# Gated cross-attention block: attention written out and prepared group by group, its values and softmax sums in 32-column tiles, the first router moved into the attention

## The reference

```
x = x + tanh(g_xattn) * attention(layernorm(x), ctx)     # 16 heads of 8 features, softmax over the 77 context tokens
x = x + tanh(g_ffn)   * moe(layernorm(x))

def moe(cur):                                            # 4 rounds, 4 experts, 2 of them weighted per token
    for r in range(4):
        logits = cur @ Wg[r] + bg[r]
        cw     = softmax over the two largest logits, 0 for the other experts
        hmid   = gelu(cur @ W1[e] + b1[e])               # 128 -> 512, for each expert e
        y      = hmid @ W2[e] + b2[e]                    # 512 -> 128
        cur    = cur + sum over e of cw[e] * y[e]
```

## Time and profile before

| | us |
|---|---|
| median of 3 runs (lowest, highest) | 546.52 (546.14, 546.67) |
| the profiled execution, its time | 545.69 |
| its span, first to last instruction | 544.0 |
| busy PE, DVE, ACT, POOL | 498.3, 408.1, 370.6, 79.0 |

### The profile page before, as it was taken

How to read it: one execution, slowest core, us unless ns; L and a number is a source line. 1 busy time by engine, 2 the same in 40 slices (tenths; PEclk the granted TensorE clock), 3 DMA queues, 4 the chain that set the end, 5 groups by cost and what they waited for, 6 DMA issues and landing times.

```text
span 544.0 us, 8396 instructions
## 1 busy us (share of the span) xinstructions
PE 498.3 (92%) x2529; PEld 401.7 (74%) x2529; DVE 408.1 (75%) x792; ACT 370.6 (68%) x717; POOL 79.0 (15%) x149
## 2 busy tenths in 40 slices
PE   0967989999679999999999999999999999999996
PEld 0845777777568788878878887887888788788884
DVE  3789888988955887786688778768877876876775
ACT  1434566556466788597778859777885977787873
POOL 3375565664400000000000000000000000000000
PEclk9985999999988999999999999999999999999999
DMA  5500000000004040021003001200400120040001
GB/s 133 162 2 0 2 0 0 0 0 0 2 0 157 0 157 1 1 77 80 2 1 155 2 0 69 89 2 0 157 1 1 74 84 0 1 175 2 19 1 39
DMA packets 13063, 22.39 MB, mean 41 GB/s; under 512 B 5200, under 2 KB 9957, under 8 KB 10981
## 3 DMA queue, kind: packets, MB, share of 16 engines
q1 hardware_dynamic: 9648, 21.42, 10.8%
q10 hardware_dynamic: 3381, 0.55, 0.6%
HBM read 20.79 MB, written 1.18 MB: 40 GB/s over the span
## 4 chain that ended last, share of the span: by engine, by line
PE 68%; DVE 13%; ACT 9%; issue 6%; DMA 2%; ACTq 1%; DVEq 0%
PE ps L1121 8%; PE ps L1123 8%; PE ps L1122 8%; PE ps L1103 8%; PE ps L1102 8%; PE ps L1101 8%; PE ps L1015 7%; ACT g_sb L590 4%; DVE h_lo L801 4%; PE ps L993 4%; PE ps L1002 3%; ACT h_hi L597 2%; ACT probT L507 2%; DMA rows_in<-in_L_xattn_bkv_dram 1%; PE ps L949 1%
## 5 line engine op out<-in xcount | busy, mean ns | idle before, releaser
L801 DVE TENSOR_TENSOR h_lo<-g_sb,h_hi 128x512 fp32r<-128x512 f32 x256 | 170.5, 688 | 88.1 <-ACT h_hi L597 88.1
L590 ACT ACTIVATE g_sb<-ps,cols 128x512 f32<-128x512 f32 x256 | 174.7, 689 | 60.4 <-PE ps L1103 60.0
L597 ACT ACTIVATE h_hi<-g_sb 128x512 fp32r<-128x512 f32 x256 | 154.8, 634 | 0.0
L1121 PE MATMUL ps<-h_hi,w_hi 128*128 128x512 f32 x256 | 103.3, 404 | 0.0
L1101 PE MATMUL ps<-x_hi,w_hi 128*128 128x512 f32 x256 | 101.9, 398 | 0.8 <-DVE x_lo L795 0.8
L1103 PE MATMUL ps<-x_hi,w_lo 128*128 128x512 f32 x256 | 102.1, 399 | 0.0
L1123 PE MATMUL ps<-h_hi,w_lo 128*128 128x512 f32 x256 | 102.0, 399 | 0.0
L1102 PE MATMUL ps<-x_lo,w_hi 128*128 128x512 f32 x256 | 101.4, 396 | 0.0
L1122 PE MATMUL ps<-h_lo,w_hi 128*128 128x512 f32 x256 | 101.3, 396 | 0.0
L811 DVE SCALAR_TENSOR_TENSOR contrib<-ps,cols,cwb 128x512 f32<-128x512 f32 x64 | 47.8, 746 | 13.6 <-PE ps L1123 8.4
L1101 PEld LDWEIGHTS ps<-x_hi,w_hi 128*128 128x128 f32 x256 | 48.5, 189 | 12.4 <-issue 1.0
(11 more groups left out here) (129 smaller groups left out, 503.3 us busy)
## 6 DMA issues: line engine op xcount, KB each, us to landing
cwb<-cw_rows SPq DMA_DIRECT2D x16, 1024.0 KB, 5.9
x_sb<-in_x_dram SPq DMA_DIRECT2D x4, 256.0 KB, 9.1
w_in<-in_L_ffn_W_dram SPq DMA_DIRECT2D x1, 1024.0 KB, 8.0
out_dram<-xn SPq DMA_DIRECT2D x4, 256.0 KB, 2.3
ctx_sb<-in_ctx_dram ACTq DMA_DIRECT2D x1, 462.0 KB
cw_rows<-cwT SPq DMA_DIRECT2D x8, 16.0 KB, 1.4
wq_in<-in_L_xattn_Wq_dram SPq DMA_DIRECT2D x1, 64.0 KB, 2.7
bv_row<-in_L_xattn_bkv_dram ACTq DMA_DIRECT2D x1, 64.0 KB, 9.7
```

The lines of the kernel that those rows point to most:

```text
L590: nc.scalar.activation(g_sb[:, k, :], ps[:, k, :], ACT.Gelu_apprx_tanh, bias=b1_c[:, e * NF + k:e * NF + k + 1]).then_inc(gelu_done, 1)
L597: nc.scalar.activation(h_hi[:, u % 2, k, :], g_sb[:, k, :], ACT.Copy).then_inc(hi_done, 1)
L801: nc.vector.tensor_tensor(h_lo[:, u % 2, k, :], g_sb[:, k, :], h_hi[:, u % 2, k, :].bitcast(F32), ALU.subtract).then_inc(lo_done, 1)
L1121: mm(yb, w2_hi[:, w], hh, start=k == 0, stop=False)
```

## The change

- Preparation goes by groups of four sequences. Only group 0 is prepared ahead; the work for group c = 1, 2, 3 is dealt out over the four iterations b of the group before (r = b % 4): r = 0 transposes of `ctx`; r = 1 K and the transposes of the normalised x; r = 2 Q and a third of V; r = 3 the other two thirds of V. Second normalisations, their transposes, `split_x` of groups 0 and 1 and the whole first router stand in iterations 5 to 15.
- V no longer goes through `pick`: PE multiplies `ctxT` (each row twice) by 16 columns of the weights per head group, four 64-column float32 matmuls for each of three row chunks (`project_v`, new L995), and DVE masks 256 columns into `v_st` (`stage_v`, new L686).
- A head group of 308 score columns has three chunks of 103, 103 and 102 rows: 12 transposes a sequence. Values and softmax sums are 24 float32 matmuls a sequence, each of 32 columns, into a column tile of its own (`weigh_values`, new L1041 and L1046; the sums use the 0/1 matrix `row_head`). The reduction, the small reciprocal, the widening, its transpose and its copy are gone; in their place is one reciprocal of 128 columns (new L710).
- The loop is written out, and the pipeline is one sequence shorter on DVE: iteration b shifts the scores of b and normalises b-1.
- SP loads the first group of x ahead of the projection matrices; ACT's queue loads `rows_in` (with one row more) ahead of `ctx`, which is in four parts. POOL adds the output bias to x sequence by sequence. The expert part is as before, but for the router of units 8 to 15, which is up to two units later, and all later copies of router weights, one unit later.

```diff
-            with pe.Fori(1, B // 2 - 1) as j:
-                attend(2 * j, 0)
-                attend(2 * j + 1, 1)
...
+            for b in range(B):
+                c, r = b // TC + 1, b % TC
+                if b + 1 < B:
+                    scores(b + 1, 0)
+                if b >= 1:
+                    weigh_values(b - 1)
+                transpose_probs(b, 0)
...
+                if c < NC:
+                    if r == 0:
+                        transpose_ctx(c)
+                    if r == 1:
+                        project_k(c)
+                    if r == 2:
+                        project_q(c)
+                    if r == 3:
+                        project_v(c, 1)
+                if b + 1 < B:
+                    scores(b + 1, 1)
+                transpose_probs(b, 1)
+                transpose_probs(b, 2)
+                if b >= 1:
+                    project_o(b - 1)
...
+                if c < NC:
+                    if r == 1:
+                        transpose_xn(c)
+                    if r == 2:
+                        project_v(c, 0)
+                    if r == 3:
+                        project_v(c, 2)
+                if r == TC - 1 and c >= 2:
+                    transpose_x(c - 2)
+                if b == B - 3:
+                    logits(0)
+                if b == B - 1:
+                    transpose_weights(0)
```

```diff
+            def weigh_values(b):
...
+                for k in range(KC):
+                    n = rows_of[k]
+                    for q in range(NQ):
+                        mm(acc(b)[32 * q:32 * q + 32, 0:L], v_st[0:n, c % 2, k, b % TC, q, :],
+                           probT[0:n, KC * q + k, :], start=k == 0, stop=k == KC - 1)
+                for k in range(KC):
+                    n = rows_of[k]
+                    for q in range(NQ):
+                        t = mm(acc(b)[32 * q:32 * q + 32, L:2 * L], row_head[0:n, k, :, :].rearrange("p h d -> p (h d)"),
+                               probT[0:n, KC * q + k, :], start=k == 0, stop=k == KC - 1)
+                t.then_inc(pv_done, 1)
```

DVE in the new iteration (its waits: `low_q` for ACT's `q_hi`, `stage_v` for PE's V, `normalise_o` for `pv_done`):

```diff
+                shift(b, 0)
+                if b >= 2:
+                    add_residual(b - 2)
...
+                if c < NC and r == 2:
+                    low_q(c)
+                if c < NC and r == 3:
+                    stage_v(c, 1)
+                shift(b, 1)
+                if b >= 1:
+                    normalise_o(b - 1)
...
+                if c < NC and r == 2:
+                    stage_v(c, 0)
+                if c < NC and r == 3:
+                    stage_v(c, 2)
+                if r == 3 and 1 <= c < NC - 1:
+                    moments(0, c + 1)
+                if r == 1 and c >= 2:
+                    moments(1, c - 2)
+                if r == 0 and c >= 3:
+                    split_x(c - 3)
...
+                if r == 0 and c < NC:
+                    normalise(0, c)
+                if r == 2 and c >= 2:
+                    normalise(1, c - 2)
+                if b == B - 3:
+                    router(0)
+                if b == B - 2:
+                    weights(0)
```

More of the change, by code:

```diff
@@ new lines, in flamingo_gated_block, with next_job, moved @@
+        turn = [0]
+        def next_job(key, reader):
+            job(key, reader, TB + turn[0] % 2)
+            turn[0] += 1
+        for b in range(B):
+            first, second = between(b)
+            next_job(("PT", b, 0), "act")
+            for key, reader in first:
+                next_job(key, reader)
+            next_job(("PT", b, 1), "act")
+            next_job(("PT", b, 2), "act")
+            for key, reader in second:
+                next_job(key, reader)
+        def moved(eng, key):
+            reader, n = jobs[key][1:3]
+            if reader == "act":
+                eng.wait_ge(job_act, n)
+            elif reader == "dve":
+                eng.wait_ge(job_dve, n)
+            elif reader == "router":
+                eng.wait_ge(gate_step, 2)
+            else:
+                eng.wait_ge(cwT_moved, 1)
@@ L708, in _, with shift @@
             mx_v = mx[:, :].rearrange("p (q h) -> p q h", q=NQ)
-            def shift(b, half, first=False):
+            def shift(b, half):
                 two = slice(2 * half, 2 * half + 2)
@@ L760, in _ @@
-            moved(dve, JOBS - 1)
-            dve.wait_ge(xres_step, 2)
-            shift(0, 0, first=True)
-            shift(0, 1, first=True)
-            attend(0, 0, values=False, residual=False)
-            attend(1, 1, residual=False)
-            with dve.Fori(1, B // 2 - 1) as j:
-                attend(2 * j, 0)
-                attend(2 * j + 1, 1)
-            attend(B - 2, 0, queries=False)
-            attend(B - 1, 1, scores=False, queries=False)
-            for c in range(NC - 1):
-                dve.wait_ge(x1_done, TC * (c + 1))
-                moments(x1_sb, 1, c)
@@ L887, in finish @@
                     op0=ALU.mult, op1=ALU.add).then_inc(fin_done, 1)
[L889 to L891 removed]
+            moments(0, 0)
+            dve.wait_ge(c_ready, 3)
+            nc.vector.tensor_reduce(head_mask[:, :], head_at[:, :, :].rearrange("p q h -> p h q"), AX.X,
+                                    ALU.add).then_inc(headmask_ready, 1)
+            normalise(0, 0)
+            moments(0, 1)
+            moved(dve, "COLS")
+            low_q(0)
@@ L982, in scores, with transpose_ctx @@
-            def scores(b, s, half, first=False):
+            tr(bank("W")[:, 0:P], wq_in[:, :], ident[:, :])
+            tr(bank("W")[0:C, P:2 * P], wk_in[:, :], ident[:, :])
+            tr(bank("W")[0:C, 2 * P:3 * P], wv_in[:, :], ident[:, :])
+            tr(bank("W")[:, 3 * P:4 * P], wo_in[:, :], ident[:, :]).then_inc(job_mm, 1)
+            pe.wait_ge(rows_ld, 16 * 5)
+            tr(bank("COLS")[:, 0:NCOL], rows_in[:, :], ident[0:NCOL, 0:NCOL]).then_inc(job_mm, 1)
+            def transpose_ctx(c):
+                key = ("CTX", c)
+                claim(key)
+                pe.wait_ge(ctx_ld[c], 16)
+                for t in range(TC):
+                    m = tr(bank(key)[0:C, t * M:(t + 1) * M], ctx_sb[:, TC * c + t, :], ident[0:M, 0:M])
+                m.then_inc(job_mm, 1)
@@ L984, in scores @@
+            passes = ((q_hi, k_hi), (q_hi, k_lo), (q_lo, k_hi))
+            def scores(b, half):
+                c, at = b // TC, slice(b % TC * L, b % TC * L + L)
                 if half == 0:
-                    pe.wait_ge(q_lo_done, b + 1)
+                    moved(pe, ("Q", c))
                     pe.wait_ge(k_stage, 3 * b + 3)
-                if not first:
+                if b >= 1:
                     pe.wait_ge(sub_done, 2 * b - 1 + half)
-                passes = ((q_hi, k_hi), (q_hi, k_lo), (q_lo, k_hi))
```

973 lines of the change are left out of this document (457 added, 516 removed).

## The result

| | us |
|---|---|
| before, median (lowest, highest), 4 runs | 546.33 (545.48, 546.67) |
| after, median (lowest, highest), 4 runs | 595.03 (592.66, 597.88) |
| ratio, 95% interval | 1.0896 (1.0846 to 1.0946) |
| profiled execution of after, its time and span | 592.66, 590.9 |
| first maximum, before and after | 41.87, 17.02 |

The change makes the kernel 9% slower. The forecast was 598. The page of the kernel after: busy times, then the rows of busy tenths and of the granted clock in 40 slices of 14.8 us.

A forecast was written before the change was run, and what follows sets the result against it. PE was busy 92%, DVE 75%, but in-order waits were taken to decide. Span 544.0, plus 37.1 for a later `up(2)` and 15 for slow clock, gave 596; with execution and median offsets, 598 us, range 560 to 645.

The forecast's parts named there:

- The mechanism: Attention loop: DVE waits for b-1's products before `shift(b + 1, 0)`, so nothing of it hides PE; 10.5 us per sequence, not 6.0.
- V = 2.8: Attention: a sequence's 24 column-tile products of values and sums take 2.8 us, overlapping only at tile borders.
- the signs named ahead: Attention trace: DVE idle before three operations, DVE and PE under 70%, iterations 7 to 9 or 12 to 14 us, `up(0)` near 192.
- The start: Before the attention: `rows_in` lands at 14.35, first maximum begins at 22.7 instead of 41.87; gain 19 us.
- The rival of tiles wholly at once: Attention values: four column tiles fully overlap, 1.4 us a sequence; time 577, or 562 without slow clock; chance 0.25.
- about 2.0: Attention values: by the skill's 2.38 gain for three column tiles, about 2.0 us a sequence, sum some 12 us lower.
- The reciprocal: Attention, DVE: the new 128-column reciprocal takes 1.0 us, from a slope giving 0.8 to 1.2.
- The clock: Attention: PE waits drop it to 1.2 GHz for a fifth of its chain, 15 us; bounds none to 74.
- the forecast's chain: Start through attention to `up(2)`: serial waits and operations at full clock put `up(2)` at 203.5, 37.1 later than before.
- The tail: Experts from `up(2)` on: both kernels do the same, 5.96 us a unit; later router weights cost nothing.
- The other side: Attention: queues do not bind, each sequence costs the fullest engine's 7.1 us; `up(2)` at 149, time 529; chance 0.10.
- the turning point: Attention: below a mean of 8.1 us an iteration, `up(2)` would come before 166.4 and the change be faster.

The follow-up runs named there:

- e7: After with preparation evictions behind `shift` halves, first router behind `shift(14, 0)`, and 57 unused PE products where PE idles ahead of scores: 530.38 us.
- e2: After with `low_q` and all `stage_v` evictions moved behind the halves of `shift` on DVE, PE's program unchanged: 548.26 us.
- e5: After with only the evictions ahead of `shift(b, 1)` (`low_q`, `stage_v(c, 1)`, `stage_v(0, 0)`) moved behind it: 573.68 us.
- e6: After with only the evictions ahead of `shift(b + 1, 0)` (`stage_v(c, 0)`, `stage_v(c, 2)`, `stage_v(0, 1)`, `stage_v(0, 2)`) moved behind it: 569.97 us.
- e1: After in its own order, with 94 extra unused float32 products on PE where it waits for DVE: 576.53 us.
- e9: e7 with `weights(0)` moved behind `shift(15, 1)` and 2 in place of 6 unused products at b = 14: 529.12 us.
- e3: After with the two loops of `weigh_values` exchanged, so one column tile's products follow each other: 601.44 us in one run.
- e10: e7 with the two loops of `weigh_values` exchanged, one column tile at a time, clock held: 545.43 us.

## Why the prediction held, step by step

The forecast of 598 lies 0.5% above 595.03, and its direction and place were right. Its sum was less good than that: errors of 28 us one way met 33 the other way.

**The mechanism: right.** The forecast said that nothing of `shift(b + 1, 0)` hides PE, since DVE cannot go past what waits for PE, and that r = 2 and 3 would be the long iterations. Predicted and measured, b = 0 to 14:

| | |
|---|---|
| predicted, full clock, V = 2.8 | 13.2 6.6 13.7 13.4 8.0 7.9 13.9 13.4 8.8 7.9 13.9 12.2 7.7 12.9 9.5 |
| after | 14.9 6.9 17.2 16.5 8.2 8.0 16.4 15.7 9.0 8.4 18.0 14.6 7.2 11.9 11.3 |
| e7 | 6.7 10.5 11.5 8.0 6.5 6.4 9.3 8.0 8.4 6.4 10.1 6.9 7.9 6.8 10.7 |

The pattern is the predicted one, and e2, e5 and e6 show the reason: move the waits, and 47 us go, clock included. Of the signs named ahead these were there: DVE idle ahead of the reciprocal, `low_q` and `stage_v`, DVE under 70% in every stage, and `up(0)` later than 192 (209.44). Two were not: PE's busy share reaches 76% in one stage, as slow products count in full, and the iterations with r = 2 and 3 last 14.6 to 18.0 us and not 12 to 14.

**The start: 5.7 too late.** 22.7 predicted, 17.02 measured. The weights' transposes start at 6.13 and not at the 11.50 of before, and the transpose of `rows_in` at 7.14; the step took that row's landing, 14.35, as what everything waits for. But the change also puts `rows_in` ahead of `ctx` in its queue. `wo_in`, which the first transpose waits for, landed 2.8 us after its issue in place of 8.8; why isn't shown.

```profile
6.13 0.44 PE L946 MATMUL ps<-ident,wq_in 128*128 128x128 f32 x1 [6.13 <-DMA wo_in<-in_L_xattn_Wo_dram]
...
7.14 0.30 PE L951 MATMUL ps<-ident,rows_in 23*128 23x23 f32 x1
```

**V: 2.8 predicted, 1.45 measured; 20 us too much** (1.35 times 15). The step held that two records of one product in the same column tile keep the next tile waiting. In the order the kernel has, four tiles in turn, they do not: 48 records in 1.45 us. The rival of tiles wholly at once (1.4, chance 0.25) had the size of this term right. Its times, 577 and 562, were still wrong, since its clock term was the forecast's own. How much of the gain is overlap is open: with one tile at a time the group takes 2.51, already under half of 24 products at the 0.24 of a full-width one (5.76), and no run has a 32-column product alone. Only the step from 2.51 to 1.45, a factor of 1.7, is shown to come from the four tiles in turn. The Trainium skill ("TensorE: Matmul & The Clock Gate", Measured speedup vs the span model) has 2.38 for three column tiles of 512 columns; against 5.76 these rows give 4.0 for four tiles in turn and 2.3 for one tile at a time. The forecast's "about 2.0" by that page is loose: 5.7 divided by 2.38 is 2.4, an estimate from that page's figure, and both lie above the measured 1.45.

**The reciprocal: 1.0 predicted, 0.952 measured.** The slope from 16 columns was good.

**The clock: 15 us predicted, some 35 to 40 left over.** With the measured start and V the forecast's chain gives `up(2)` at 203.5 - 5.7 - 20.2 = 177.6; it came at 220.57, 43 us later. Some 3 of them are `normalise`, priced at 1.03 and about that (1.10 to 1.11) in iterations 0, 4, 8 and 14, but not in 6 and 10, where POOL works at the same time:

```profile
102.02 3.15 DVE L670 TENSOR_SCALAR xn<-x_sb,mv,rstd 128x128 f32<-128x128 f32 x4
...
153.98 2.32 DVE L670 TENSOR_SCALAR xn<-x_sb,mv,rstd 128x128 f32<-128x128 f32 x4
```

With them the chain's `up(2)` is 181. The other 40 are clock, and whatever else the chain had too small. e1 shows 18.5 to be clock at least, and by the estimate above some 35. Single iterations say the same: b = 3 and 11, predicted 12.05 and 10.85 with the measured V, took 12.0 and 10.8 in e1 at full clock and 16.5 and 14.6 in after; b = 9, predicted 6.55, took 6.4 in e7 at 1.00 and 8.4 in after at 0.50. So the chain was right there, and the difference is clock. A fifth of PE's chain was taken as slow. With a mean granted clock of 0.72 over 20 to 180, between the 0.50 and 1.00 of the two levels, more than half of the time was at 1.2 GHz, and it may be more: in iteration 1, 33.50 to 40.39, the view grants 1.00, but 24 records of the values last 1.51 there, as at 0.50, and not the 0.86 of full clock. The row used for a fifth, 6.10 of 8.90 us busy at clock 1.00, was a stretch of 9 us behind a busy one, and not 150 us in which PE waits again and again. The rows of r = 2 suggest that the slow clock also feeds itself (slower products lengthen DVE's wait, and so PE's), but no run shows that by itself.

**The tail: "from `up(2)` on the two kernels do the same", 7.3 too much.** The forecast counted the later router weights as nothing lost; they were 5.5 us won, since PE had waited for them seven times. The missing 1.8 was not traced further.

**Together:** -5.7 - 20.2 + 28 - 7.3 = -5, from the predicted span of 596 to 590.9; of the 28, 3 are `normalise`, and 25 are clock and whatever else is open. A range of 560 to 645 was honest about this; the point was lucky.

**The other side, 529, was real, but not this kernel.** The forecast priced the case in which queues don't bind at 529. e9, which does the same work in another order with the clock kept up by added products, takes 529.12. That the numbers are the same is luck too: its `up(2)` is 5.9 us later than the rival's 149, and the part behind it 7.2 shorter than before's. That rival put the turning point at a mean of 8.1 us an iteration, with the start at 24.3; with the earlier start e7's 8.3 already gives 158.29 for `up(2)`, and e9 has 8.1 and 154.93. What was not tried: `normalise_o(b - 1)` behind `shift(b + 1, 0)`, the place that this rival named.

## What to carry to other kernels

An operation that evicts a late product belongs behind everything in its queue that is ready, and above all behind what feeds the producer: here the place of seven calls was worth 47 us, the clock that it gave back included, with no work added or removed. Read the granted clock by stage before believing any duration, and read an unexpected small effect twice, once with the clock held; the same edit was 6 us in e3, on the change's own order at an uneven clock, and 15 in e10. Where an engine must wait anyway, products into an unused place can be worth more than they cost (12.5 us from 57 of them).

## What the runs showed of the hardware

- Four column tiles of 32 columns, float32, issued in turn, ran 48 records in 1.45 us, 0.030 a record, and one tile at a time in 2.51, 0.052 a record. At 1.2 GHz the same group took 2.72 (58.85 to 61.57):

```profile
58.85 1.51 PE L1041 MATMUL ps<-probT,v_st 103*32 103x128 f32 x24
60.13 1.51 PE L1046 MATMUL ps<-probT,row_head 103*32 103x128 f32 x24
61.57 1.18 PE L1026 MATMUL ps<-ident,prob 128*103 128x128 f32 x4
```

- DVE's reciprocal takes 0.952 us for 128 columns and 0.253 for 16, 6.2 ns a column, over three times the 0.291 of a product of two 128-column operands. The larger one reads PSUM and the smaller one SBUF.
- The granted clock fell to 0.59 in after's stage of 100 to 140, where PE waits twice in each iteration with r = 2 or 3, and stayed at 1.00 in e7's, where unused products stand in such waits. A clock term taken from a short stretch behind a busy one was too small by more than half.
- DVE's `normalise`, four operations from SBUF to SBUF, took 1.10 to 1.11 us in four of after's iterations, with no POOL instruction beside it, and 3.15 and 2.32 us the two times that POOL's products and subtractions ran at the same time. No run takes POOL's work away, so the cause is argued from the two lanes of the timeline.
